# Last mixture of experts: one region of sorted rows and 23 tiles a pass, with the first addition of the mixing on GpSimd

## The reference, cut to what matters

```python
def _L3_ffn_ref(tgt, Wr, br, W1, b1, W2, b2, gamma, beta):      # 8 experts, D = 128, F = 512
    logits = jnp.einsum('bsd,ed->bse', tgt, Wr) + br
    top_v, top_i = jax.lax.top_k(logits, 2)
    top_w = jax.nn.softmax(top_v, axis=-1)
    router_w = jnp.sum(jax.nn.one_hot(top_i, n_exp) * top_w[..., None], axis=-2)
    h = jax.nn.relu(jnp.einsum('bsd,efd->bsef', tgt, W1) + b1)
    o = jnp.einsum('bsef,edf->bsed', h, W2) + b2
    return _layer_norm(tgt + jnp.einsum('bsed,bse->bsd', o, router_w), gamma, beta)
...
x = x + 0.5 * _L3_ffn_ref(_layernorm(x), ...)
x = x + _L3_attn_ref(_layernorm(x), ...)
x = x + 0.5 * _L3_ffn_ref(_layernorm(x), ...)
```

## Time and profile before

| | |
|---|---|
| median of 3 runs | 3111.8 us (3108.44 to 3114.26) |
| the profiled execution's own time | 3112.1 us |
| its span in the profile | 3110.4 us |
| busy share of TensorE, VectorE, ScalarE, GpSimd | 85%, 72%, 55%, 30% |
| mean granted TensorE clock | 0.934 of 2.4 GHz |
| first low part of the first pass and of the second | 2405.7 us, 2836.6 us from the span's start |
| last addition to `x_res` | 3107.2 us |

### The profile page before, as it was taken

The page is one execution under the profiler, slowest core; times in us unless marked ns, Lnnn a source line. Parts: engine busy times, 40 slices in busy tenths (PEclk is TensorE's granted clock), DMA queues, the critical chain, the costliest instruction groups (busy, mean ns, idle before and its releaser), DMA issues. The chain is left out here.

```text
span 3110.4 us, 41720 instructions
## 1 busy us (share of the span) xinstructions
PE 2657.2 (85%) x13086; PEld 1624.1 (52%) x13086; DVE 2226.2 (72%) x5317; ACT 1695.8 (55%) x2926; POOL 928.1 (30%) x1099
## 2 busy tenths in 40 slices
PE   7998888989899999878998967878888998765984
PEld 5776432333377766434655533333555776654762
DVE  5565777878466578677876678788687768776675
ACT  4443476767644444575444467675343785314862
POOL 1011234333200000121000057667245217354045
PEclk8999999999999999998999978988998999767996
DMA  5802112221012133101233333222244674004762
GB/s 144 169 11 75 39 58 73 63 68 55 30 61 87 53 104 100 42 0 48 97 93 117 114 92 95 82 83 85 69 118 154 212 234 163 15 26 161 240 225 94
DMA packets 142211, 299.22 MB, mean 96 GB/s; under 512 B 23420, under 2 KB 35772, under 8 KB 134184
## 3 DMA queue, kind: packets, MB, share of 16 engines
q1 hardware_dynamic: 132216, 276.88, 28.9%
q0 software_dynamic: 8192, 16.79, 1.8%
q10 hardware_dynamic: 1584, 2.88, 0.3%
HBM read 245.96 MB, written 70.94 MB: 102 GB/s over the span
## 5 line engine op out<-in xcount | busy, mean ns | idle before, releaser
L482 POOL TENSOR_TENSOR norm_rstd<-norm_rstd,minus_half 128x4 f32<-128x4 f32 (+1 forms) x136 | 167.3, 1230 | 1101.5 <-DVE norm_rstd L469 1090.6
L1055 DVE TENSOR_REDUCE gate_scratch<-banks 128x2 f32<-128x1024 f32 (+2 forms) x320 | 344.8, 1113 | 92.6 <-PE banks L300 64.3
L1215 ACT ACTIVATE main_tiles<-banks 128x512 f32<-128x512 f32 (+1 forms) x608 | 314.8, 581 | 130.7 <-PE banks L1196 88.7
L309 PE MATMUL banks<-main_tiles_r,ffn_weights 128*128 128x512 f32 x560 | 229.1, 409 | 10.3 <-DVE main_tiles_r L750 6.0
L2853 POOL DMA_INDIRECT main_tiles<-sorted_rows_d,token_rows x128 | 139.8, 1092 | 291.3 <-DMA sorted_rows_d<-mamba_tiles 226.0
L311 PE MATMUL banks<-main_tiles_r,ffn_weights 128*128 128x512 f32 x560 | 222.6, 397 | 0.0
L310 PE MATMUL banks<-main_tiles_r,ffn_weights 128*128 128x512 f32 x560 | 222.5, 397 | 0.0
L1232 POOL TENSOR_SCALAR_AFFINE_SELECT main_tiles<-main_tiles 128x128 f32<-128x128 f32 (+2 forms) x352 | 119.7, 344 | 285.8 <-ACT main_tiles L1215 280.7
L309 PE MATMUL banks<-main_tiles_r,moe_weights 128*128 128x512 f32 x380 | 179.7, 473 | 8.3 <-DVE main_tiles_r L2960 3.7
L2952 ACT ACTIVATE main_tiles_r<-banks,tile_bias 128x512 fp32r<-128x512 f32 x192 | 132.5, 690 | 90.7 <-PE banks L311 79.0
L2312 ACT ACTIVATE main_tiles<-banks 128x512 f32<-128x512 f32 x144 | 84.7, 598 | 163.5 <-PE banks L311 153.3
(11 more groups left out here) (446 smaller groups left out, 7308.2 us busy)
## 6 DMA issues: line engine op xcount, KB each, us to landing
main_tiles<-gates_d SPq DMA_DIRECT2D x272, 256.0 KB, 3.2
moe_weights<-w_parts_d SPq DMA_DIRECT2D x60, 1024.0 KB, 5.1
mamba_tiles<-c_rows_d SPq DMA_DIRECT2D x92, 256.0 KB, 3.4
sorted_rows_d<-in_zero SPq DMA_DIRECT2D x6, 3328.0 KB, 44.9
mamba_tiles<-sorted_rows_d SPq DMA_DIRECT2D x60, 256.0 KB
sorted_rows_d<-mamba_tiles SPq DMA_DIRECT2D x60, 256.0 KB, 4.3
spare_nat<-c_rows_d SPq DMA_DIRECT2D x36, 256.0 KB, 3.4
found_d<-main_tiles SPq DMA_DIRECT2D x32, 256.0 KB, 2.0
```

Of the source, the lines that this page charges most:

```text
L309: eng.matmul(o, wh, hi, start=first, stop=False)
L482: eng.tensor_tensor(rstd[:, k, 1, 0:w], rstd[:, k, 0, 0:w], minus_half[:, 0:w], ALU.pow).then_inc(s.norm_pow)
L1055: eng.tensor_reduce(o.rearrange("p (n s) -> p s n", s=2)[:, :, j0:j0 + per], psum[:, b0:b0 + 2, 0:per * (k1 - k0)].rearrange("p s (n c) -> ...
L1215: eng.activation(weight_tile(u)[:, 0:width], psum[:, score_at[u], 0:width], ACT.Exp, scale=HD ** -0.5).then_inc(s.at_exp)
```

## The change

Both groups of a pass now share one region, in which each expert has 8 blocks, and a pass has 23 tiles. After chunk 5 the program knows that at least 5 blocks are full; these are the tiles of the first list (`dve_first_table`, `FULL_TILES` = 5). All other tiles (18) are listed after chunk 7 (`dve_rest_table`), in the order in which chunks become complete: the blocks that hold rows of chunks 0 and 1 first, then those up to chunk 3, and so on. For that the counts after chunks 1, 3, 5 and 7 are held (`tile_counts`). The gathers of a pair of chunks now wait for the store of tile 15, 17, 19 or 23 (`DONE_AFTER`) in place of the end of their group (19 or 30 before). The semaphores of the scatters stay apart: `sent` of chunks 0 to 5 lets the first 5 tiles go, that of chunks 6 and 7 the other 18.

In the mixing, L3012's four instructions leave VectorE. GpSimd does their work in two: it weighs all second rows of a chunk, then adds the kept rows (`pool_m3_mix`).

The two regions together have 142 blocks in place of 78, and the clears are 8 of 4544 KB in place of 6 of 3328 KB. The planned times of the linear attention move by 8 us against the last tile, and those of its norms are written anew. `dve_first_table` has 21 small steps, `dve_rest_table` 19, five of them over 18 x 31 numbers; the chunks 1 and 3 have 2 steps more than before.

```diff
+FULL_TILES = (2 * C * 6 - E8 * (C - 1) + C - 1) // C
+TILES3 = (2 * T + E8 * (C - 1)) // C
+PASS_BLOCKS = 2 * T // C // 2 * E8 + E8 - 1
+DONE_AFTER = (15, 17, 19, 23)
...
-    CLEAR_ROWS = SPARE_BLOCKS * C // S * P // 6
+    CLEARS = 8
+    CLEAR_ROWS = SPARE_BLOCKS * C // S * P // CLEARS
...
-        for k in range(6):
-            yield 100.0 + 20.0 * k
+        for k in range(CLEARS):
+            yield 100.0 + 25.0 * k
...
+    def totals(cc):
+        return cc % 2 == 1
...
+            if c == 5:
+                yield from dve_first_table(eng, p, at_ + 4.4, step)
+                step += FIRST_STEPS
+            elif c == 7:
+                yield from dve_rest_table(eng, p, at_ + 4.4, step)      # 19 steps, 5 of them over 18 x 31 numbers
+            else:
+                eng.tensor_tensor(over_grid, every_expert(), over_limits("thr"), ALU.is_gt).then_inc(s.g3_step)
+                yield at_ + 4.8
+                eng.wait_ge(*since("g3_step", step + 1))
+                eng.tensor_reduce(blocks_upto(c // 2), over_grid, AX.X, ALU.add).then_inc(s.g3_step)
...
+        for c in range(NC_ * p, NC_ * p + NC_):
+            at_ = max(starts[DONE_AFTER[c % NC_ // 2] - 1] + 30.0, at_ + 11.0)
+            mix_at.append(at_)
...
-    def stored(G):
-        last = GROUPS3[G].tile0 + GROUPS3[G].tiles
+    def stored(cc):
+        last = TILES3 * (cc // NC_) + DONE_AFTER[cc % NC_ // 2]
         return since("y_out0", 16 * ((last + 1) // 2)), since("y_out1", 16 * (last // 2))
...
     def dve_m3_mix(eng):
         for cc, c, G, when in m3_chunks(mix_at):
-            yield when
-            eng.wait_ge(got[cc % 2], 128 * (cc // 2 + 1))
+            yield when + 1.6
             one, two = picked(cc, 0), picked(cc, 1)
-            for t in range(TPC):
-                sl = slice(t * TILE, (t + 1) * TILE)
-                z = eng.scalar_tensor_tensor(out=two[:, sl], in0=two[:, sl], scalar=wts[:, c, 1, t:t + 1], in1=kept(c)[:, sl],
-                                             op0=ALU.mult, op1=ALU.add)
-            z.then_inc(s.mix_half)
-            yield when + 1.6
-            eng.wait_ge(*since("mix_half", cc + 1))
+            eng.wait_ge(*since("mix_half", 2 * cc + 2))
...
+    def pool_m3_mix(eng):
+        for cc, c, G, when in m3_chunks(mix_at):
+            yield when - 1.2
+            eng.wait_ge(got[cc % 2], 128 * (cc // 2 + 1))
+            eng.wait_ge(*since("g3_step", gate3_base(cc) + GATE3_STEPS))
+            two = picked(cc, 1)
+            parted = two.rearrange("p (t d) -> p t d", d=TILE)
+            eng.tensor_tensor(parted, parted, wts[:, c, 1, :].unsqueeze(2).broadcast_to([P, TPC, TILE]),
+                              ALU.mult).then_inc(s.mix_half)
+            eng.wait_ge(*since("mix_half", 2 * cc + 1))
+            eng.tensor_tensor(two, two, kept(c), ALU.add).then_inc(s.mix_half)
...
-    LA_NORMS = (-33.0, -23.0, -11.0, -1.0, 17.0, 26.4, 42.1, 45.3)
+    LA_NORMS = (-23.0, -12.0, -1.0, 10.0, 21.0, 32.0, 43.0, 54.0)
     T_LA = m3_tiles[-1][0] + TILE3_US + 6.0
-    la_at = [T_LA + LA_US * b for b in range(NB)]
+    la_at = [T_LA + 8.0 + LA_US * b for b in range(NB)]
```

More of the change, by code:

```diff
@@ L1655, in pe_gates3 @@
             cc = key[1]
-            first = group_of(cc).first == cc
+            first = cc % NC_ == 0
             yield when
@@ L1776, in dve_gates3 @@
             assert step == begin + GATE3_STEPS
-            if not closes(cc):
+            if not totals(cc):
                 continue
             ranks += 1
-            K, J, side = group.count, group.tiles, group_no(cc) % 2
-            of_expert, of_tile, of_bias = [P, E8, K], [P, J, E8], [P, J, 4, E8]
-            over = g3_t[:, 0:E8 * K].rearrange("p (e k) -> p e k", k=K)
-            flags = g3_t[:, 0:E8 * J].rearrange("p (j e) -> p j e", e=E8)
-            small = E8 * J
-            expert, begins = g3_t[:, small:small + J], g3_t[:, small + J:small + 2 * J]
-            table = g3_t[:, small + 2 * J:small + 4 * J].rearrange("p (k j) -> p k j", k=2)
-            needs, upto = g3_t[:, small + 4 * J:small + 4 * J + E8], g3_t[:, small + 4 * J + E8:small + 4 * J + 2 * E8]
-            iota = rowv[:, ROWS["iota"]:ROWS["iota"] + J]
             yield at_ + 4.4
@@ L1816, in dve_gates3 @@
-            eng.tensor_tensor(begins, iota, begins, ALU.subtract).then_inc(s.g3_step)
-            yield at_ + 7.6
-            eng.wait_ge(*since("g3_step", step + 8))
-            eng.scalar_tensor_tensor(out=begins, in0=expert, scalar=float(K), in1=begins, op0=ALU.mult,
-                                     op1=ALU.add).then_inc(s.g3_step)
-            yield at_ + 8.0
-            eng.wait_ge(*since("g3_step", step + 9))
-            eng.tensor_scalar(table[:, 0, :], begins, float(group.base), None, ALU.add).then_inc(s.g3_step)
@@ L1839, in dve_gates3 @@
-            yield at_ + 10.0
-            eng.wait_ge(*since("g3_step", step + 15))
-            first = g3_t[:, small:small + J * 4 * E8].rearrange("p (j f e) -> p j f e", f=4, e=E8)
-            eng.tensor_tensor(first, flags.unsqueeze(2).broadcast_to(of_bias),
-                              colv[:, COLS["l3b1"]:COLS["l3b1"] + 4 * E8].rearrange("p (e f) -> p f e", f=4).unsqueeze(1)
-                              .broadcast_to(of_bias), ALU.mult).then_inc(s.g3_step)
-            yield at_ + 10.8
@@ new lines, in build, with every_expert, over_limits @@
+    over_grid, full_grid = [g3_t[:, k:k + E8 * E8].rearrange("p (e k) -> p e k", k=E8) for k in (0, E8 * E8)]
+    wide = gr_t.rearrange("p n c -> p (n c)")
+    segments = 4 * E8 - 1
+    turn = rowv[:, ROWS["turn"]:ROWS["turn"] + segments]
+    small = MAX_TILES * segments
+    def every_expert():
+        return psum[:, 7, 352:352 + E8].unsqueeze(2).broadcast_to([P, E8, E8])
+    def over_limits(name):
+        return rowv[:, ROWS[name]:ROWS[name] + E8].unsqueeze(1).broadcast_to([P, E8, E8])
@@ new lines, in dve_tile_bias @@
+    def dve_tile_bias(eng, side, J, expert, at_, step):
+        of_tile, of_bias = [P, J, E8], [P, J, 4, E8]
+        flags = g3_t[:, 0:E8 * J].rearrange("p (j e) -> p j e", e=E8)
+        second = g3_t[:, E8 * J:2 * E8 * J].rearrange("p (j e) -> p j e", e=E8)
+        first = g3_t[:, E8 * J:5 * E8 * J].rearrange("p (j f e) -> p j f e", f=4, e=E8)
+        eng.tensor_tensor(flags, rowv[:, ROWS["index"]:ROWS["index"] + E8].unsqueeze(1).broadcast_to(of_tile),
+                          expert.unsqueeze(2).broadcast_to(of_tile), ALU.is_equal).then_inc(s.g3_step)
+        yield at_ + 0.4
+        eng.wait_ge(*since("g3_step", step + 1))
+        eng.tensor_tensor(second, flags, colv[:, COLS["l3b2"]:COLS["l3b2"] + E8].unsqueeze(1).broadcast_to(of_tile),
+                          ALU.mult).then_inc(s.g3_step)
+        yield at_ + 0.8
+        eng.wait_ge(*since("g3_step", step + 2))
+        eng.tensor_reduce(b2t[:, side, 0:J], second, AX.X, ALU.add).then_inc(s.g3_step)
+        yield at_ + 1.2
+        eng.wait_ge(*since("g3_step", step + 3))
+        eng.tensor_tensor(first, flags.unsqueeze(2).broadcast_to(of_bias),
+                          colv[:, COLS["l3b1"]:COLS["l3b1"] + 4 * E8].rearrange("p (e f) -> p f e", f=4).unsqueeze(1).broadcast_to(of_bias), ALU.mult).then_inc(s.g3_step)
+        yield at_ + 2.0
+        eng.wait_ge(*since("g3_step", step + 4))
+        eng.tensor_reduce(b1t[:, side, 0:J, :], first, AX.X, ALU.add).then_inc(s.g3_step)
@@ L2845, in pool_got @@
                 if n == 0:
-                    for sem, value in stored(G):
+                    for sem, value in stored(cc):
                         eng.wait_ge(sem, value)
```

216 lines of the change are left out of this document (134 added, 82 removed).

## The result

The kernel after the change takes 3092.7 us in the median of 4 runs (3089.5 to 3095.8), the kernel before 3111.2 beside it: a ratio of 0.9940, with a 95% interval of 0.9923 to 0.9958. It is faster by 0.6%, and the forecast was 3090. The profiled execution took 3089.5 us in all, 22.6 less than that of before, and the medians lie 18.4 apart; the sum had said 22.4. That the sum is so near is partly luck, as the steps show.

The account below looks back on a forecast made before the run. Bound by the first gather's start, the mixing loop's pace and, between the passes, the linear attention. Clears +4, the second pass's earlier start -21.7 and the second pass itself -4.7 gave -22.4 from 3112.1: 3089.7 us, range 3055 to 3123.

Parts of the forecast that it names:

- Term 2: Mixing loop's pace: GpSimd's two new operations and part of a landing wait slow each chunk by 3.0 us.
- d: Slowdown of the mixing loop per chunk from GpSimd's new work: 3.0 us, with bounds 0 and 5.
- Rival A: Mixing loop: GpSimd's new work fits in the loop's waits (d at most 1), 3060 us; chance 0.18.
- Term 1: First gather waits for an earlier tile's store: 18.5 us earlier in the first pass, 27.2 in the second.
- Term 3: Linear attention between the passes: batch 2's first step moves to 2690.4, so the second pass starts 21.7 us earlier.
- Term 5: Larger clears hold up the shift's store: 0 to 7 us late, and all behind it; taken as +4.
- B: All tile time is given back, 95 us, to 3017, with TensorE bounding to the end; chance 0.04.
- D: Time between the passes doesn't move, as gates or attention hold; about no change, 3111 us; chance 0.08.
- Rival C: Mixing loop: GpSimd's two operations and VectorE's hold each other up; d = 6 gives 3132 us; chance 0.14.

Follow-up runs that it names:

- experiment 2: Seven more tiles, on blocks nobody reads, at the second pass's end: on the kernel after 3117.1 us, on after with the mixing back on VectorE 3076.0 us.
- Experiment 3: The kernel after with tile 5's first-pass loads moved ahead of one store: 3080.6 us; or with tile 5 planned 6.4 us behind tile 4: 3078.5 us.
- six kernels of the table: Before 3111.2 us, after 3092.7, after with mixing on VectorE 3052.7, before with mixing on GpSimd 3138.5; both after kernels with 30 second-pass tiles 3117.1 and 3076.0.
- after's repetition: The kernel after run once more, unchanged: 3093.0 us in the median of 6 runs, ratio 0.9947 to the kernel before.

## Why the prediction was right, step by step

The profiled executions, with what each step was said to give:

| step | predicted | measured |
|---|---|---|
| up to the first low part | +4 | +0.1 |
| from there to that of the second pass | -21.7 | -12.4 |
| second pass, to its eighth combine | -4.7 | -10.5 |
| eighth combine of the second pass | -22.4 | -22.9 |

**Term 2, the new work's price, was right as a whole.** The operations took 1.03 and 1.26 us (1.27 each predicted), the landing cost 1 us a chunk in the mean (16.0 us in 16 chunks; 0.5 predicted), and GpSimd's old waits took part of it in. I said d = 3.0; with the same tiles it is 3.2 in the second pass of after and 1.8 in the first. The fourteen periods give 35 us, and the medians 40, against 14 d = 42. Rival A (it fits in the waits) falls. The Trainium skill, "GPSIMD Engine Reference", section "Engine selection", puts GpSimd about 2x behind VectorE on two-input work. The trace agrees: GpSimd's addition of 128x512 took 1.26 us, and VectorE's subtraction of that shape, both inputs in SBUF (L3046), 0.68. The whole step went from 1.14 us in four fused operations to 2.29 in two.

**Term 2, the base pace, was wrong.** I took 14.9 and 14.2 us from before and said that the dropped tiles "give nothing by themselves: they ran inside the loop's waits". They did not: experiment 2 prices them at 2.5 to 2.9 us each. Behind the tile that frees the first gather stand 8 tiles now and stood 11. With the mixing as before, the seven periods fall from 14.2 to 12.7 us in the second pass and from 16.2 to 15.1 in the first (my 14.9 was of the first five alone): 10.6 and 8.2 us that I left out. Three tiles at the price of experiment 2 are 7.6 to 8.7 of them. With the move on top, the periods of after are 16.9 and 15.9 us, where I said 17.9 and 17.2; I had called myself wrong at a pace under 16, and in the second pass it is.

**Term 1: right in kind.** The first gather of the second pass comes 21.1 us sooner after its first tile (27.2 predicted), because the first 14 tiles take 101.2 us where the same took 95.4 before. I had seen the longer table as covered by tile 5's wait, and took nothing off for it in the second pass. There it stands on VectorE among the first tiles, five such steps close together (558 numbers each), and tile 2's low part comes 9.8 us behind tile 1's, not 7.7:

```profile
2831.30 0.69 DVE L2998 TENSOR_TENSOR mamba_tiles_r<-banks,mamba_tiles_r 128x512 fp32r<-128x512 f32 x1 [0.49 <-ACT mamba_tiles_r L2991]
...
2834.27 0.73 DVE L1889 TENSOR_TENSOR gate_scratch<-gate_scratch,row_consts 128x558 f32<-128x558 f32 x1
...
2841.11 0.68 DVE L2998 TENSOR_TENSOR mamba_tiles_r<-banks,mamba_tiles_r 128x512 fp32r<-128x512 f32 x1
```

The block can't be all of the 5.8 us: tiles 2 and 3 hold 3.2 of them, and 2.4 come at tiles 10 and 14, where VectorE waited 2.1 us for TensorE (L3088) each time. No run takes the table out, so its price isn't shown. In the first pass tile 5 was 11.9 us late and not 8.7: ahead of its loads in SyncE's queue stood the store of tile 3, which I did not look at. Experiment 3 shows it.

**Term 3: right place, wrong size.** Batch 2's first step came at 2691.8 (2690.4 and the clears' 4 predicted), 16.6 us behind the eighth combine where it was 25.8. But "from batch 2 on ... as before" failed: the next two batches took 4 us longer each, and the second pass begins 148 to 150 us behind the eighth combine in all six kernels of the table. What the new order gained ahead of batch 2 was lost behind it. TensorE's granted clock in these two batches is 0.66 and 0.60, against 0.76 and 0.69 before, so nearer to its lower level of 1.2 GHz, and its transposes L452 (L450 in before) are longer in the mean, and ten more. Before and after:

```profile
L450 PE MATMUL banks<-const_mats,x_res 128*128 128x128 f32 x20 | 3.4, 299 | 2.2 <-DVE normed_pairs L556 2.2
L452 PE MATMUL banks<-const_mats,x_res 128*128 128x128 f32 x30 | 7.0, 372 | 1.9 <-ACT attn_tiles L547 1.2 <-DVE normed_pairs L558 0.6
```

From 2600 to 2620 and from 2620 to 2640 us TensorE was busy for 10 of 20 us each, at 0.59 and 0.76, where it was for 16 at 0.91 and 0.99 before: fewer tiles are left there. The clock goes with the loss, but it isn't shown to be the cause. In after's repetition the second of these batches had 0.67, near the 0.69 of before, and was as long as in after (37.6 us up to its last addition, 38.0 in after, 34.5 before). TensorE idled as long in the two batches as before (22 and 23 us); it was busy 8.6 us more, with 283 matmuls in place of 266, and its three costliest groups together took no longer (26.8 and 27.3 us). The gates' steps also stand otherwise among these batches: TensorE waited 9.8 us for VectorE's marks L1745, and 2.6 before. No run parted clock, order and the added matmuls. The kernel with the mixing back has the same long batches (40.4 and 41 us), so the mixing's move isn't the cause.

**Term 5: right mechanism.** The eighth clear held the shift's store, which took 11.0 us to land, where that of before took 3.1. It was issued 2.5 us earlier and so landed 5.5 us later, and the scores came at 346.0, 3.9 us later as predicted. In the order of the trace:

```profile
332.37 0.33 SPq L1136 DMA_DIRECT2D shift_d<-gate_scratch  x1
343.42 1.25 SPq L1141 DMA_DIRECT2D q_stacks<-shift_d  x2
```

"All behind it" was wrong: of 5.9 us at 366 there were 2.4 left at 530, 1.8 at 1437 and none at 2405.

So the errors nearly cancel. In the first stretch 5.7 us more came by the eighth combine than I said (2675.2 against 2680.9), and 15.1 us less from there to the second pass; in the second pass the forgotten 10.6 us of pace and 2.9 at the first combine stand against 6.1 of term 1 and 1.5 of d; and the clears' 4 us weren't lost. Rivals **B** and **D** fall too: the tiles' time was not all given back, and the time between the passes did move, by 12.4 us. **Rival C** did not come: the additions took at most 1.59 us and mostly 1.26 beside VectorE. Its price, though, is what the move costs against doing without: with the tiles as they were, the same move alone made the kernel 26 us slower.

## What to carry to other kernels

A change that bundles a gain with a loss can land on its forecast and still leave the loss to be taken back: price each part alone. Here everything but the move (the 23 tiles, the earlier gathers, the new order) was worth some 59 us, and the move of the mixing to GpSimd cost 40 of them. GpSimd, which issues the indirect DMAs, was full at a busy share of 68%; add the gaps between the issues and the wait for their landing to such a stream before you give it more work. And work that runs beside a bound loop isn't free: count what it adds to the loop's landings and to the queue of the engines that the loop passes through.

## What was not expected of the hardware

- A gap of 0.30 us stands between two gathers and one of 1.1 us between a power and the gather behind it, but only 0.15 behind the addition L3112. With them, a chunk's stream is 12.3 of the 12.7 us of a period, on an engine that is 30% busy over the whole program.
- With tiles beside them, gathers took 1.15 us in place of 1.04 in the mean (63.5 and 57.0 us for 55) and landed in 3.1 us in place of 2.6 in the median.
- A clear of 4544 KB among other loads of its queue cost the program 8 to 10 us (25 us for three in the medians, 32 in the profile), and three of them some 2 us where the queue was empty. A small store right behind one took 11.0 us to land, where the same store took 3.1.
